# Four prologue loads on ScalarE's queue, banks per half for the first group, mask splitting into the last group of the loop, down weights scaled on GpSimd

## What is computed

```python
x = x + tanh(g_xattn[0]) * wkv(time_decay, time_first, layernorm(x), ctx)      # a scan over the tokens
x = x + tanh(g_ffn[0])   * ffn(layernorm(x))          # silu(x@gate_w*gate_s) * (x@up_w*up_s) @ down_w * down_s
x = x + tanh(g_xattn[1]) * attention(layernorm(x), ctx, mask)    # 16 heads of 8, masked softmax
x = x + tanh(g_ffn[1])   * moe(layernorm(x))          # top-1 of 8 experts with capacity, plus a shared expert
```

## Time and profile before

| | us |
|---|---|
| median of 3 runs (lowest, highest) | 587.51 (583.6, 588.49) |
| the profiled execution, its own time | 581.58 |
| span of the profiled execution, first to last instruction | 579.8 |
| first block: feed-forward products begin | 43.27 |
| loop, g = 1: from the first of its feed-forward products to that of g = 2 | 80.31 to 114.39 |
| second block's first VectorE instruction | 149.24 |

### The profile page before, as it was taken

The page is one execution under the profiler, slowest core; times in us unless marked ns, Lnnn a source line. Parts: engine busy times, 40 slices in busy tenths (PEclk is TensorE's granted clock), DMA queues, the critical chain, the costliest instruction groups (busy, mean ns, idle before and its releaser), DMA issues. The chain is left out here.

```text
span 579.8 us, 10728 instructions
## 1 busy us (share of the span) xinstructions
PE 487.7 (84%) x3400; PEld 269.2 (46%) x3400; DVE 397.8 (69%) x871; ACT 243.7 (42%) x478; POOL 217.8 (38%) x353
## 2 busy tenths in 40 slices
PE   1149999999696769899988888888779999899994
PEld 1034564747353424333343343333233555578883
DVE  4989879695336778888888888887755733333331
ACT  1132233121231048777777777777741001123331
POOL 2526234231283235555555555531301370024334
PEclk9999999999997969999999999999899999999998
DMA  5901007630267054655555555450004024157873
GB/s 139 334 2 36 1 6 119 88 43 0 73 179 191 20 135 131 154 157 145 140 154 144 144 145 144 125 128 5 5 2 149 32 105 138 55 126 194 195 151 36
DMA packets 68246, 61.94 MB, mean 107 GB/s; under 512 B 8992, under 2 KB 63248, under 8 KB 68208
## 3 DMA queue, kind: packets, MB, share of 16 engines
q1 hardware_dynamic: 65136, 57.25, 37.8%
q0 software_dynamic: 3072, 4.21, 4.3%
HBM read 39.01 MB, written 22.43 MB: 106 GB/s over the span
## 5 line engine op out<-in xcount | busy, mean ns | idle before, releaser
L1008 DVE TENSOR_REDUCE MX<-psum 128x2 f32<-128x512 f32 x256 | 166.3, 681 | 31.6 <-PE psum L874 31.5
L1086 ACT ACTIVATE HP<-psum 128x512 f32<-128x512 f32 x256 | 138.6, 600 | 43.6 <-PE psum L880 42.9
L874 PE MATMUL psum<-QKA 60*128 60x256 bf16 x512 | 82.0, 279 | 18.3 <-DVE MX L1008 16.7
L880 PE MATMUL psum<-QKA 60*128 60x256 bf16 x512 | 80.0, 277 | 9.4 <-ACT HP L1086 7.4
L953 PE MATMUL psum<-HP,VP 128*32 128x256 f32 x1024 | 82.9, 397 | 0.2 <-ACT HP L1086 0.2
L437 PE MATMUL psum<-space_a,space_w 128*128 128x512 f32 x160 | 72.8, 606 | 4.1 <-PEq L497 2.4
L874 PEld LDWEIGHTS psum<-QKA 60*128 60x128 bf16 x512 | 35.3, 95 | 64.9 <-DVE MX L1008 47.8
L1656 POOL DMA_INDIRECT out_x<-OE,to_u x16 | 25.0, 1562 | 72.6 <-ACT OE L1697 70.2
L437 PEld LDWEIGHTS psum<-space_a,space_w 128*128 128x128 f32 x160 | 29.8, 193 | 40.4 <-issue 34.4
L1795 PE MATMUL psum<-XT,WE 128*128 128x256 f32 (+1 forms) x192 | 44.1, 380 | 1.6 <-ACT XT L1681 1.6
L1721 PE MATMUL psum<-space_a,wsh 128*128 (+3 forms) x96 | 42.8, 595 | 0.8 <-PEq L1224 0.8
(11 more groups left out here) (183 smaller groups left out, 739.8 us busy)
## 6 DMA issues: line engine op xcount, KB each, us to landing
QKA<-stack_scr SPq DMA_DIRECT2D x32, 480.0 KB, 5.4
stack_scr<-PARTS SPq DMA_DIRECT2D x32, 192.0 KB, 2.1
WE<-in_W SPq DMA_DIRECT2D x16, 352.0 KB, 4.0
stack_scr<-PARTS SPq DMA_DIRECT2D x32, 128.0 KB, 1.9
XD<-dispatched SPq DMA_DIRECT2D x8, 258.0 KB, 3.7
X<-in_x SPq DMA_DIRECT2D x4, 512.0 KB, 5.5
CV<-in_ctx SPq DMA_DIRECT2D x4, 512.0 KB, 3.6
CX<-in_ctx SPq DMA_DIRECT2D x16, 128.0 KB, 5.1
```

Of the source, the lines that this page charges most:

```text
L874: return pe.matmul(to[:, tt * T:(tt + 1) * T], QKA[rows, k, 0, h, tt * P:(tt + 1) * P], QKA[rows, k, 1, h, :], start=True, stop=True)
L880: return pe.matmul(to[:, (j % 2) * T:(j % 2 + 1) * T], QKA[rows, k, 1, h, st * P:(st + 1) * P], QKA[rows, k, 0, h, :], start=True, stop=True)
L1008: dve.tensor_reduce(MX[:, par, head_of(n), :], src[:, :].rearrange("p (a s) -> p a s", a=2), axis=AX.X, op=ALU.max).then_inc(a_red, 1)
L1086: act.activation(PT[:, i % 2, st, 2 * half:2 * half + 2, :].rearrange("p j t -> p (j t)"), TBK3[THIRDS[m]], ACT.Exp).then_inc(a_exp, 1)
```

## The change

It edits the first block in six ways.

1. Four small loads (time_decay, time_first, the two gates) are issued on ScalarE's queue with a semaphore `s_chain` of their own; ScalarE and VectorE wait for these alone. The other eleven go behind the context load of group 1 on SyncE's queue; x of group 1 gets its own semaphore and goes ahead of the weights.
2. In group 0 the second half uses banks 2 and 3 (`WB2`) rather than those of the first half, so TensorE does not wait for the exponentials and products of the first half.
3. The mask split moves from the prologue into the last group of the loop.
4. The scaling of the down weights moves from VectorE to GpSimd, between the sums and the quotients of group 0.
5. The scaling of wq and bq moves from the prologue to the end of the last group.
6. In all groups the reciprocal of half 0 of the next group stands behind `dve_h` of slice 0 rather than ahead of `dve_h1` of slice 0.

SyncE's code for the fourteen stores and the wait behind them is as before.

```diff
-            WB = [bank[4], bank[5]]
+            WB, WB2 = [bank[4], bank[5]], [bank[2], bank[3]]
...
                 @block.scalar
-                    act.wait_ge(s_ld, 16 * N_SMALL)
+                    chain = [(td[:], time_decay), (tf[:], time_first),
+                             (gates[:, 0:2], g_xattn.partition_broadcast(P)), (gates[:, 2:4], g_ffn.partition_broadcast(P))]
+                        for dst, src in chain:
+                            act.dma_start(dst, src).then_inc(s_chain, 16)
+                    act.wait_ge(s_chain, 16 * N_CHAIN)
...
                 @block.gpsimd
                     for h in range(2):
                         pool_sums(pool, 0, h)
+                    pool.wait_ge(s_wts, 80)
+                    pool.wait_ge(s_ld, 16 * N_SMALL)
+                    pool.tensor_tensor(dw[:, :, :], dw[:, :, :], dsb[:, :].unsqueeze(1).broadcast_to([P, NI, C]),
+                                       ALU.mult).then_inc(s_dw, 1)
                     for h in range(2):
                         pool_quot(pool, 0, h)
...
                 @block.vector
                     def dve_group(ch, g, last):
-                        dve_recip(dve, g + 1, 0)
                         for i in range(NI):
                             dve_h1(dve, ch, g, i)
                             dve_h(dve, ch, g, i)
                             if i == 0:
+                                dve_recip(dve, g + 1, 0)
                                 dve_products(dve, g + 1, 1)
                                 dve_scans(dve, g + 1, 1)
                             if i == 1 and not last:
                                 dve_stats1(dve, ch, g + 2)
+                            if i == 1 and last:
+                                mask_lines()
+                                mask_part(0)
                             if i == 2:
                                 dve_recip(dve, g + 1, 1)
+                            if i == 3 and last:
+                                mask_part(1)
                             if i == 4:
                                 dve_x1(dve, g + 1)
                         dve_ln2(dve, ch, g + 1)
                         if not last:
                             dve_products(dve, g + 2, 0)
                             dve_scans(dve, g + 2, 0)
+                        else:
+                            mask_part(2)
+                            mch.do(dve.tensor_scalar(wq[:], wq[:], HD ** -0.5, None, ALU.mult))
+                            mch.do(dve.tensor_scalar(bqk[:, 0:1], bqk[:, 0:1], HD ** -0.5, None, ALU.mult))
                         dve_x2(dve, g, DB)
```

More of the change, by code:

```diff
@@ L282, in flamingo_kernel, with later, pe_wkv_in @@
             s_x2 = primed("s_x2")
-            WB = [bank[4], bank[5]]
+            WB, WB2 = [bank[4], bank[5]], [bank[2], bank[3]]
             DB = [bank[6], bank[7]]
             after_wkv = []
-            def pe_wkv_in(pe, g, h):
+            def later(count):
+                return not isinstance(count, int) or count > 0
+            def pe_wkv_in(pe, g, h, WB=WB):
                 n = 2 * g + h
@@ L507, in load_ctx @@
                         sp.dma_start(CV[:, :, :], ct[:, bass.ds(GB * g, GB), :]).then_inc(s_c, 16)
[L509 to L523, removed]
+                    load_x(0)
+                    load_ctx(0)
+                    sp.dma_start(mrow[:], mask).then_inc(s_mask, 16)
+                    load_x(1, s_xb)
                     sp.dma_start(gw[:, :, :], gate_wT.rearrange("(h p) i -> p h i", p=P)).then_inc(s_wts, 16)
@@ L531, in _ @@
                     load_ctx(1)
-                    for g in range(1, NG):
+                    small = [(gs[:, 0:NI - 1], gate_s[0:(NI - 1) * P].rearrange("(i p) -> p i", p=P)),
+                             (us[:, 0:NI - 1], up_s[0:(NI - 1) * P].rearrange("(i p) -> p i", p=P)),
+                             *[(dst[HALF_I * f:HALF_I * (f + 1), NI - 1:NI], src[(NI - 1) * P:INTER].rearrange("(p a) -> p a", a=1))
+                               for dst, src in ((gs, gate_s), (us, up_s)) for f in range(2)],
+                             (dsb[:], down_s.partition_broadcast(P)), (bvb[:], bv.partition_broadcast(P)),
+                             (bqk[:, 0:1], bq), (bqk[:, 1:2], bk), (wq[:], wqT)]
+                    assert len(small) == N_SMALL
+                    with nc.allow_non_contiguous_dma(reason="small vectors"):
+                        for dst, src in small:
+                            sp.dma_start(dst, src).then_inc(s_ld, 16)
+                    for g in range(2, NG):
                         load_x(g, s_xr)
@@ L650, in _ @@
                     last.then_inc(s_mT, 1)
[L651 to L654, removed]
+                    pe_wkv_in(pe, 0, 0)
+                    pe_wkv_in(pe, 0, 1, WB2)
+                    pe_wkv_out(pe, 0, WB2)
                     pe_wkv_in(pe, 1, 0)
                     pe_z2T(pe, 0)
+                    pe.wait_ge(s_wts, 80)
                     def pe_group(g, last):
@@ L683, in _ @@
                     dve_z1(dve, 0)
[L684 to L699, removed]
+                    dve.wait_ge(s_chain, 16 * N_CHAIN)
                     dve.tensor_scalar(upos[:], tf[:], 0.0, -1.0, ALU.max, ALU.mult).then_inc(s_dv0, 1)
                     dve.tensor_scalar(uneg[:], tf[:], 0.0, None, ALU.min).then_inc(s_dv0, 1)
-                    dve.tensor_scalar(hgs[:], gs[:], 0.5, None, ALU.mult).then_inc(s_dv0, 1)
-                    dve.wait_ge(s_dv0, 3)
-                    ch.do(dve.tensor_tensor(hgu[:], hgs[:], us[:], ALU.mult))
+                    dve.wait_ge(s_mT, 1)
+                    dve.tensor_copy(maskT[:, :, :].rearrange("p h b -> p (h b)"), bank[7][:, 0:2 * B]).then_inc(s_mT2, 1)
                     dve.wait_ge(s_act0, 3)
@@ L733, in dve_group, with mask_part @@
+                    def mask_part(r):
+                        mch.wait()
+                        last = dve.tensor_copy(mparts[:, :, r, :], mtmp[:, :, :])
+                        if r == 2:
+                            last.then_inc(s_mp, 1)
+                            return
+                        mch.do(last)
+                        mch.wait()
+                        mch.do(dve.tensor_tensor(mtmp[:, :, :], mtmp[:, :, :], mparts[:, :, r, :], ALU.subtract))
                     def dve_group(ch, g, last):
-                        dve_recip(dve, g + 1, 0)
@@ L842, in at @@
                     return g + (k + ahead) // GB, (k + ahead) % GB
-                def later(count):
-                    return not isinstance(count, int) or count > 0
                 def pe_proj_k(pe, g, k):
```

60 lines of the change are left out of this document (34 added, 26 removed).

## The result

| | before | after |
|---|---|---|
| median of 4 runs each (lowest, highest), us | 586.49 (583.6, 588.49) | 619.23 (618.3, 620.23) |
| ratio of the medians, 95% interval | | 1.0563 [1.0511, 1.0614] |
| span of the profiled execution, us | 579.8 | 617.0 |
| feed-forward products of group 0 begin | 43.27 | 40.29 |
| the same of g = 1, of g = 2 | 80.31, 114.39 | 77.98, 113.86 |

The change makes the kernel slower by 32.7 us in the medians. The spans differ by 37.2, since the execution that was profiled before was 4.9 us shorter than its median, and the one after 0.5 us shorter than its own.

What follows compares the result with a forecast made beforehand. TensorE bounds the loop, a chain of single steps the prologue; late, uncovered mask stores (145.0 + 37.7) and 0.9 us put the next block at 183.6, not 149.24. That 34.4 us on 585.5 gives 620 us, range 608 to 627.

Steps and rivals of the forecast that it cites:

- the third reading: SyncE's queue at the first block's end: mask stores take 37.7 us, and its 25.7 us wait is all their cover.
- the stores drain at the pace of other transfers: Rival, mask stores: at 259 GB/s they take 12 us, next block at 157.9, total 594 us; chance 0.06.
- the block's end doesn't hold the others: Rival, first block's end: SyncE alone waits for the stores, only VectorE's 3.3 us shift counts, 589 us; chance 0.06.
- GpSimd as the bound of the prologue: Rival, prologue: scaling takes 6.3 us or longer, or loads land late; gain 1 us or nothing, 623 us; chance 0.20.
- In g = 0 nothing is lost: Loop, g = 0: the reciprocal moved behind slice 0 costs nothing, since VectorE enters late there.
- cost at nothing: Ahead of the loop: scalings of down weights and wq leaving VectorE's list count 0, as the moved reciprocal replaces them.
- The reciprocal behind slice 0: Loop, g = 1: the moved reciprocal makes the group 1.5 us longer; the last group starts its scans as late.
- The sign forecast for it: Profile after, g = 1: TensorE's wait for Y would be longer by 1.5 us.
- Loads and banks: Prologue: four loads of its own let ScalarE start sooner, PA 3.1 us earlier; the second half's banks win nothing more.
- Mask part 1: Prologue: without it, addition X ends 2.9 us behind Y (2.0 transposes, 0.75 second half), at 31.7.
- Mask work in the last group: Last group, VectorE: 2.6 and 2.2 us of mask work, less 1.0 of gaps; with the reciprocal's 1.5, Z2 5.3 later.
- A page against a row: Store pace: the profile's 88 GB/s used over the skill's line rate at 512 bytes and 104 GB/s from 16 partitions.

Runs made afterwards that it cites:

- e1: Changed kernel with the mask split back at its old places in the prologue: 587.85 us against 585.58 for the kernel before, ratio 1.0038.
- e2: Kernel before with only the mask split moved into the last group: 618.65 us, ratio 1.0563.
- e4: Changed kernel with the reciprocal of half 0 back ahead of slice 0 in all groups, mask split still late: 613.84 us, ratio 1.0458.
- e7: e5 with the down weights scaled on VectorE, behind the mask, rather than on GpSimd: 582.9 us, ratio to the kernel before 0.9955.
- e6: e5 with one pair of banks for both halves of group 0: 581.88 us in one run, against 580.99 for e5.
- e5: e4 with the mask operations set in gaps of VectorE's prologue: 580.99 us against 585.19 for the kernel before, ratio 0.9921.
- e10: Changed kernel with the two stores of constants read from 48 and 96 partitions rather than 16: 612.79 us, one run.
- e8: Changed kernel with the fourteen stores shared between the queues of SyncE and ScalarE: 621.19 us, one run.

## Why the prediction was right, and where its terms were off

**What bounds the kernel, and the third reading.** The step that decided, "the 25.7 us are all the cover they have", held. e1 and e2 isolate it from both sides: without the late mask the loss is 2.3 us, with it alone 33.1 (618.65 - 585.58).

**The rivals.** That the stores drain at the pace of other transfers failed: 37.2 us, with nothing beside them. That the block's end doesn't hold the others failed: 31 us of idle time on VectorE, gone in e1. GpSimd as the bound of the prologue came true only in that the eleven loads were late: the scaling took 3.42 us (I took 3.8) but started at 24.07 and not 22.5, and 2.98 us of gain were left where the rival had 1 or none.

**The terms, in us at the second block's start:**

| term | predicted | measured |
|---|---|---|
| prologue | -3.5 | -2.98 |
| reciprocal in g = 0 | 0 | +0.65, with the rest of that stretch |
| reciprocal in g = 1 | +1.5 | +1.80 |
| last group to Z2, with the reciprocal and two mask parts | +5.3 | +5.94 |
| first store | 145.0 | 147.07 |
| the stores | 37.7 | 37.2 |
| from the last landing to the next block | 0.9 | 0.4 |
| next block | 183.6 | 184.7 |

*In g = 0 nothing is lost* was wrong. "VectorE enters late there" is true of the kernel before, where the scalings kept VectorE until 47.86; the change takes them off VectorE's list, and VectorE then stood idle for 3.49 us before slice 0, time in which e4 runs the reciprocal. By e4 its new place costs 1.25 us or more there, of which 0.6 comes back (e4's g = 0 is 36.44 us long, 37.04 before). I read that 0.6 as the two scalings, which I had "cost at nothing"; no run tries them alone, but with that of the down weights back on VectorE g = 0 is 1.7 us longer (e7).

*The reciprocal behind slice 0* in g = 1 came out near its size (+1.80 for +1.5), and Y came later by it as forecast. The sign forecast for it did not come: TensorE's wait for Y is 0.91 us, as before (0.88); the delay shows ahead of it, as the 1.44 us for HP of slice 1.

*Loads and banks*: the loads, put near 7 ("tg near 7"), came 2.7 us later, but the gain did not hang on them: ScalarE still waited 0.83 us for Z1's transposes before the first exponential, and PA was 0.4 us later than the 12.2 that the 3.1 implies. The banks were put at nothing, and e6 shows nothing of them on VectorE's list.

*Mask part 1*: 2.0 and 0.75 are 2.75, not 2.9; from the end of Y to that of the addition it took 2.81. *Mask work in the last group* was short by 0.6: the three lines took 1.49 us beside GpSimd's NUM where they took 0.68 in the prologue. Together the four terms make the first store 2.1 us late, and the drain and the barrier give 1.0 of it back.

**The rest of the program.** I took nothing for TensorE's slower start after 30 us without work. The granted clock in the gap, from 158 us on, is 0.50, the lower of the two levels (1.2 of 2.4 GHz), and the first four products took 3.75 us where the same four took 1.96 in the profile before. The long gap is not needed for that: in e5 TensorE had waited 1.98 us, and the four took 3.65 at a granted clock of 0.52. The reason given for "nothing" held: the next products wait for one of the block's own loads, before and after:

```profile
153.31 0.70 PE L851 MATMUL psum<-CX,wk 128*128 128x256 f32 x2 [2.12 <-DMA MB<-in_mask]
```

```profile
188.66 1.22 PE L868 MATMUL psum<-CX,wk 128*128 128x256 f32 x2 [0.17 <-DMA MB<-in_mask]
```

What the four products lose comes off that wait, 2.12 us before and 0.17 after. The total shows no loss either: from the next block to the end the profiles took 430.6 (before), 432.3 (after), 430.9 (e2), 431.4 (e4) and 434.9 (e5), and e5, the longest, has no such gap. That stretch scatters by 4 us from profile to profile.

**The sum.** 620 against 619.2 is in part luck: 34.4 us were forecast, the next block moved by 35.5, the medians differ by 32.7, and their interval is some 3 us wide to each side. The range's lower bound took stores some 7 us shorter, for which no row stood; they were 0.5 us shorter.

**A page against a row.** The row gave the size rightly. The Trainium skill (DMA: Bandwidth & Descriptors, Specifications) has 512 bytes as the size for line rate; rows of 512 bytes went at 88 GB/s from 16 partitions and at 250 from 96, so row length was no guarantee here. The Trainium skill (SBUF — State Buffer, Door 1: The DMA port swizzle) has the pace follow the number of SBUF ports that the partitions reach, four for partitions 0 to 15. e10 agrees in direction, with 88 GB/s from 16 partitions where that page has 104. The Trainium skill also says (DMA: Bandwidth & Descriptors, Issuing engines are not separate DMA queues) that transfers issued on several engines run on the same sixteen DMA engines; e8's 87 GB/s on two queues agrees.

## What to carry to other kernels

Before a producer is moved later, find the last thing that it releases and measure what cover that has: stores that end 26 us ahead of a block's barrier look free, and are free only there. A gap in a list is a better place for side work than a later stage with a full engine: e5 keeps the gain of the prologue because each mask operation stands where VectorE waited anyway. And the stores from 16 partitions drained at 87 to 88 GB/s from one queue and from two: start such a transfer early, or try a source of more partitions, which made the two constant stores faster in e10.

## What the runs showed of the hardware that was not expected

- Four loads that fill 1 KB each, issued on ScalarE's queue within the first 2.65 us beside the bulk loads on SyncE's, landed 1.8, 3.4, 6.3 and 7.5 us after their issue.
- The three mask lines of 16 x 256 took 0.68 us in the prologue and 1.49 with GpSimd's NUM beside them; the subtraction of 16 x 768 took 0.94 and, beside GpSimd's sums in e5, 1.95. GpSimd's scaling of 1,536 columns took 3.42 us beside a reciprocal, 1.14 per 512 columns against the 1.26 of NUM.
- In e10, windows in which the store from 48 partitions has neighbours from 16 beside it read 106 GB/s (160.5 to 162 us) and 142 (162 to 164); the store from 96 partitions, alone, reads 250.
